# Attention scores against 64 keys instead of 128, each batch's result in a PSUM bank of its own

## The chip, the cores and the metric

The kernel runs on one core of a Trainium2 chip. The metric is the device time of one launch in microseconds (us); the number given for a kernel is the median of its runs.

## The reference, cut to what matters

The program is a GRU scan, an attention layer over the GRU's states, a Runge-Kutta integration and a quantized feed-forward layer, with residuals between them. The change lies in the attention:

```python
q = (xn @ Wq)...          # 32 batches, 16 heads, 64 positions, 128 wide
k, v = kv[..., :dh], kv[..., dh:]          # one key and value head for all 16
q, k = rotary(q) * scale, rotary(k)
sim = einsum('bhid,bjd->bhij', q, k)       # 64 x 64 for each batch and head
sim = where(causal, -max_float, sim)
attn = softmax(sim - max(sim))
out = einsum('bhij,bjd->bhid', attn, v)
```

A query meets the 64 keys of its own batch and no others.

## The kernel before, in words

Five engines run programs of their own and meet by semaphores. The stages follow one another: the GRU (0 to about 380 us of the span), attention (about 389 to 1008 us), then Runge-Kutta and feed-forward together to the end.

**Attention** goes over 8 blocks (`NBLK`) of 4 batches (`BLK_B`), 256 tokens. A block is 2 pairs (`PAIRS`) of batches, since two batches of 64 positions fill 128 partitions. All operands of its matmuls are float32, for which the profile records two weight loads and two matmuls for each `matmul` in the program. TensorE's order of work is written out by hand in `attn_block` of the tensor program. For each block:

- keys of the block (L667), values (L671), then the queries of the 16 heads (L656, 64 matmuls of 256 columns). VectorE rotates the heads as they come (L1180, L1182, L1197) into `q_rot`, laid out as batch, head, position; the rotated keys are in `kr`, 256 columns, 64 for each batch.
- `before(0)`: a quarter of the output projection of the block before (8 matmuls of 512 columns, L646, 16 records).
- `scores(0)` (L681 to L691): for each batch of pair 0, 8 matmuls, one for each pair of heads. The weights are the 128 query columns of two heads (`q_rot`), and the moving operand is 128 keys: those of both batches of the pair. A batch's 8 results fill two PSUM banks: banks 2 and 3 for the pair's first batch, 4 and 5 for its second. Half of each result (the keys of the other batch) is not used. One semaphore (`s_mm`) is raised after each batch.
- `before(1)`, then `scores(1)` into the same banks 2 to 5; for that, TensorE first waits until VectorE has read out the earlier batch of those banks (`masked`, L685).
- `turned_probs(0)` (transposes, L701), `before(2)`, `values(0)` (L714), `turned_probs(1)`, `before(3)`, `values(1)`. `values` puts its results into banks 5, 2 and 3, after all four batches of the block were read (`masked`).

In the first block there is no output projection, so the parts `before(...)` are empty.

VectorE's `softmax(blk, pr)` works on the two batches of a pair in turn: for each batch it adds the causal mask while reading the batch's own keys out of PSUM (L1213), takes the maximum (L1216), subtracts it (L1219); ScalarE takes the exponential (L936); VectorE sums (L1222), inverts (L1225) and scales (L1228), and raises `p_done`, for which `turned_probs` waits. After both pairs VectorE normalizes the next block's input (L1165, L1170) and adds the residual of the last (L1234). ScalarE copies the turned probabilities (L943) and the attention's output (L948) out of PSUM.

The read of the scores in `softmax` is this view: two banks, head by head, 64 of each 128 columns.

```python
own = ps[:, 2 + 2 * (n % 2):4 + 2 * (n % 2), :].rearrange(
    "p a (h b j) -> p (a h) b j", b=2, j=T)[:, :, n % 2, :]
```

Of the kernel before, what the change touches and what calls it, by code (L numbers as in the profile page):

```python
# [13 lines left out]
P = 128  # L14
B, T, D = 32, 64, 512
# [8 lines left out]
PAIRS = BLK_B // 2  # L24
# [113 lines left out]
def gru_attn_rk4_ffn(nc, xT, x, cond_quad, cond_T, W_ih, W_hh, gate_bias, state_bias, gamma, Wq, Wkv, Wo,  # L138
                     couplingT, bias_quad, w_gate, w_up, w_down, down_idx, ident, mean_of, trig, mask,
                     x1_scr, q_scr, wgu_scr, wd_scr, scale_scr, tok_scr, out):  # L140
    with ExitStack() as ctx:
        mem = ctx.enter_context(nc.sbuf_tensor("mem", [P, WORDS], F32))
        ps = ctx.enter_context(nc.psum_tensor("ps", [P, 8, 512], F32))
# [4 lines left out]
        def f32(a, *dims):  # L148
            n = 1
            for d in dims:  # L150
                n *= d
            v = mem[:, a:a + n]
            if len(dims) == 2:
                v = v.rearrange("p (a b) -> p a b", a=dims[0])
            if len(dims) == 3:
                v = v.rearrange("p (a b c) -> p a b c", a=dims[0], b=dims[1])
            return v
# [24 lines left out]
        q_rot = f32(a_ih, BLK_B, HEADS * T)  # L182
# [7 lines left out]
        kr, kturned = f32(w.take(BLK), BLK), f32(w.take(BLK), BLK)  # L190
# [379 lines left out]
        def _(pe):  # L570
# [67 lines left out]
            def out_proj(blk, part):  # L638

                pr, h0 = part // 2, part % 2 * HP  # L640
                if h0 == 0:

                    pe.wait_ge(x1_done, PRIMED + PAIRS * (blk - 1) + pr + 1)
                    pe.wait_ge(ao_cp, 4 * (PAIRS * blk + pr + 1))
                for h in range(h0, h0 + HP):
                    mm = pe.matmul(ps[:, 6 + pr, :], aoT[:, h, pr * P:pr * P + P], wo[:, h, :], start=(h == 0), stop=(h == HEADS - 1))  # L646
                if h0:
                    mm.then_inc(wo_mm, 1)

            def q_heads(blk):  # L650
                for h in range(HEADS):
                    if h >= Q_BANKS:

                        pe.wait_ge(q_ev, 3 * (HEADS * blk + h - Q_BANKS + 1))
                    for c in range(NC):
                        mm = pe.matmul(ps[:, h % Q_BANKS, 0:BLK], wq[:, c, h * DH:(h + 1) * DH], xnb[:, c, :], start=(c == 0), stop=(c == NC - 1))  # L656
                    mm.then_inc(q_mm, 1)

            def attn_block(blk, first):
                pe.wait_ge(xn_done, blk + 1)  # L660
                if not first:

                    pe.wait_ge(x1_done, PRIMED + PAIRS * (blk - 1))
                    pe.wait_ge(pT_cp, 2 * PAIRS * blk)
                    pe.wait_ge(ao_cp, 4 * PAIRS * blk)
                for c in range(NC):
                    mm = pe.matmul(ps[:, 7, 0:BLK], wkv[:, c, 0:DH], xnb[:, c, :], start=(c == 0), stop=(c == NC - 1))  # L667
                mm.then_inc(k_mm, 1)
                for pr in range(PAIRS):
                    for c in range(NC):  # L670
                        mm = pe.matmul(ps[:, 5, pr * DH:(pr + 1) * DH], xnb[:, c, pr * P:pr * P + P], wkv[:, c, DH:], start=(c == 0), stop=(c == NC - 1))  # L671
                mm.then_inc(v_mm, 1)
                q_heads(blk)
                pe.wait_ge(kr_done, blk + 1)

                def before(part):

                    if not first:
                        out_proj(blk - 1, part)

                def scores(pr):  # L681
                    for b2 in range(2):
                        if pr:

                            pe.wait_ge(masked, 2 * PAIRS * blk + 2 * pr - 1 + b2)  # L685
                        b = 2 * pr + b2
                        for hp in range(HP):

                            o = ps[:, 2 + 2 * b2 + hp // 4, (hp % 4) * P:(hp % 4 + 1) * P]
                            mm = pe.matmul(o, q_rot[:, b, hp * P:(hp + 1) * P], kr[:, pr * P:(pr + 1) * P], start=True, stop=True)  # L690
                        mm.then_inc(s_mm, 1)  # L691

                def turned_probs(pr):
                    pe.wait_ge(p_done, 2 * (PAIRS * blk + pr + 1))
                    for half in range(2):

                        n = 2 * pr + half
                        if n >= 2:
                            pe.wait_ge(pT_cp, 2 * PAIRS * blk + n - 1)
                        for hp in range(4 * half, 4 * half + 4):  # L700
                            mm = pe.transpose(ps[:, half, (hp % 4) * P:(hp % 4 + 1) * P], probs[:, pr, hp * P:(hp + 1) * P], identf)  # L701
                        mm.then_inc(pT_mm, 1)

                def values(pr):
                    pe.wait_ge(pT_cp, 2 * PAIRS * blk + 2 * pr + 2)

                    pe.wait_ge(masked, 2 * PAIRS * (blk + 1))
                    for half in range(2):
                        for b2 in range(2):
                            n = 4 * pr + 2 * half + b2  # L710
                            if n >= 3:

                                pe.wait_ge(ao_cp, 4 * PAIRS * blk + n - 2)
                            pe.matmul(ps[:, PV_BANKS[n % 3], :], vtok[64 * b2:64 * b2 + 64, pr, :], pT[64 * b2:64 * b2 + 64, half * 512:(half + 1) * 512],  # L714
                                      start=True, stop=True).then_inc(pv_mm, 1)
                before(0)
                pe.wait_ge(qr_done, HEADS * (blk + 1))
                pe.wait_ge(v_cp, blk + 1)
                scores(0)
                before(1)  # L720
                scores(1)
                turned_probs(0)
                before(2)
                values(0)
                turned_probs(1)
                before(3)
                values(1)
# [104 lines left out]
            for bank in range(2):  # L832

                mm = pe.matmul(ps[:, bank, 0:P], identf, mix[0], start=True, stop=True)
# [200 lines left out]
        def _(dve):  # L1035
            def bcast(row, nb):

                return row.unsqueeze(1).to_broadcast([P, nb, T])
# [160 lines left out]
            def softmax(blk, pr):  # L1199

                def of(n):
                    return probs[:, pr, :].rearrange("p (h b j) -> p h b j", h=HP, b=2)[:, :, n % 2, :]

                def row(a, n):
                    return a[:, n, :].unsqueeze(2).to_broadcast([P, HP, T])

                def at(n):
                    return 2 * PAIRS * blk + n + 1
                two = (2 * pr, 2 * pr + 1)
                for n in two:  # L1210
                    dve.wait_ge(s_mm, at(n))
                    own = ps[:, 2 + 2 * (n % 2):4 + 2 * (n % 2), :].rearrange("p a (h b j) -> p (a h) b j", b=2, j=T)[:, :, n % 2, :]
                    dve.tensor_tensor(of(n), own, bcast(masks, HP), ALU.add).then_inc(masked, 1)  # L1213
                for n in two:
                    dve.wait_ge(masked, at(n))
                    dve.tensor_reduce(smax[:, n, :], of(n), AX.X, ALU.max).then_inc(max_done, 1)  # L1216
                for n in two:
                    dve.wait_ge(max_done, at(n))
                    dve.tensor_tensor(of(n), of(n), row(smax, n), ALU.subtract).then_inc(shifted, 1)  # L1219
                for n in two:  # L1220
                    dve.wait_ge(exp_done, at(n))
                    dve.tensor_reduce(ssum[:, n, :], of(n), AX.X, ALU.add).then_inc(sum_done, 1)  # L1222
                for n in two:
                    dve.wait_ge(sum_done, at(n))
                    dve.reciprocal(ssum[:, n, :], ssum[:, n, :]).then_inc(inv_done, 1)  # L1225
                for n in two:
                    dve.wait_ge(inv_done, at(n))
                    dve.tensor_tensor(of(n), of(n), row(ssum, n), ALU.mult).then_inc(p_done, 1)  # L1228
# [7 lines left out]
            def attn_block(blk, first, last):  # L1236
                dve.wait_ge(k_mm, blk + 1)
                rotated(by_time(kr), by_time(kturned), by_time(ps[:, 7, 0:BLK]), 2, k_parts)
                dve.wait_ge(k_parts, 3 * (blk + 1))
                dve.tensor_tensor(kr, kr, kturned, ALU.add).then_inc(kr_done, 1)  # L1240
                q_out(blk)
                for pr in range(PAIRS):
                    softmax(blk, pr)
                if first:

                    dve.wait_ge(rows_ld, 32)
                if not last:
                    norm(blk + 1)
                if not first:
                    residual(blk - 1)  # L1250
# [307 lines left out]
```

## Time and profile before

| what | value |
|---|---|
| median of 3 runs | 1623.13 us (1622.98 to 1623.77) |
| the profiled execution's own time | 1630.71 us |
| its span, first to last instruction | 1628.8 us |
| TensorE matmuls (PE) busy | 1505.1 us, 92% of the span |
| TensorE weight loads (PEld) busy, beside the matmuls | 933.8 us, 57% |
| VectorE (DVE) busy | 1122.3 us, 69% |
| ScalarE (ACT) busy | 591.0 us, 36% |
| GpSimd (POOL) busy | 383.0 us, 24% |
| mean granted TensorE clock | 0.975 of full speed |

Line numbers (L690) are those of the kernel. PE stands for matmuls and PEld for the loads of their stationary operand, both on TensorE. Durations of matmuls overlap, because they are pipelined; the time that a stream of them takes is read from a stretch, not from the duration of one. "Idle" is what stood before an instruction on its engine, with what ended it. PEclk is the TensorE clock that the throttle granted: 1.0 is 2.4 GHz, 0.5 is 1.2 GHz.

### The profile page before, as it was taken

The page shows a single profiled execution, that of the slowest core. Times are in us where ns is not written, and L with a number is a line of the kernel's source. Part 1 is how long each engine was busy: PE and PEld are TensorE (multiplying, and loading weights), DVE is VectorE, ACT ScalarE, POOL GpSimd, SP SyncE. Part 2 cuts the span into 40 slices and gives each one's busy share as a digit, 9 for nine tenths or more (in the row PEclk, how much of TensorE's full clock was granted, in tenths as well). Part 3 has the DMA queues.
Part 4 walks back from the last instruction along what each step waited for, and adds up shares of the span by engine and source line. Part 5 has one row for each costly group of instructions (what it writes and reads, how often), then busy time and mean ns, then how long its engine had stood idle before and what let it go on. Part 6 is the DMA issues. An engine that isn't in the chain of part 4 may idle for free.

```text
span 1628.8 us, 46380 instructions
## 1 busy us (share of the span) xinstructions
PE 1505.1 (92%) x16624; PEld 933.8 (57%) x16624; DVE 1122.3 (69%) x3565; ACT 591.0 (36%) x1903; POOL 383.0 (24%) x545
## 2 busy tenths in 40 slices
PE   5999999996799999999999998789999999999995
PEld 1333333334675758576766753566666666666662
DVE  1676667765755747575756541578889898898886
ACT  1444445451111020202011110455655555555552
POOL 0221221120000000000000000235556655555650
PEclk9999999998889999999999999999999999999996
DMA  7111211216100000000000004201111111111111
GB/s 306 45 45 50 51 47 56 61 47 168 10 1 8 19 13 13 26 0 26 0 26 1 25 6 167 73 24 30 37 32 35 34 48 40 32 35 35 32 44 39
DMA packets 91035, 72.79 MB, mean 45 GB/s; under 512 B 32480, under 2 KB 82912, under 8 KB 89824
## 3 DMA queue, kind: packets, MB, share of 16 engines
q1 hardware_dynamic: 71184, 59.35, 12.4%
q10 hardware_dynamic: 18032, 6.88, 1.7%
q0 software_dynamic: 1760, 5.77, 1.3%
q8 instruction: 37, 0.61, 0.2%
q14 instruction: 22, 0.18, 0.0%
HBM read 55.03 MB, written 16.94 MB: 44 GB/s over the span
## 4 chain that ended last, share of the span: by engine, by line
PE 68%; DVE 14%; issue 7%; POOL 5%; ACT 4%; DMA 1%; POOLq 0%; DVEq 0%; SPq 0%; ACTq 0%
PE ps L656 14%; PE ps L646 14%; PE ps L584 11%; PE ps L596 10%; PE ps L751 7%; PE ps L690 3%; PE ps L714 3%; DVE mem L1327 2%; POOL mem L532 2%; DVE mem L1278 2%; ACT mem L969 2%; POOL mem L514 2%; PE ps L741 1%; DVE ps L1303 1%; PE ps L667 1%
## 5 line engine op out<-in xcount | busy, mean ns | idle before, releaser
L751 PE MATMUL ps<-mem 128*32 128x128 f32 x8192 | 278.8, 277 | 38.9 <-ACT mem L969 32.9
L751 PEld LDWEIGHTS ps<-mem 128*32 128x32 f32 x8192 | 211.6, 110 | 109.5 <-ACT mem L969 68.9
L646 PE MATMUL ps<-mem 128*128 128x512 f32 x512 | 224.6, 592 | 0.0
L656 PE MATMUL ps<-mem 128*128 128x256 f32 x1024 | 222.3, 379 | 0.0
L510 POOL TENSOR_TENSOR mem<-mem 128x128 f32<-128x128 f32 x64 | 39.6, 618 | 743.3 <-ACT mem L964 743.3
L656 PEld LDWEIGHTS ps<-mem 128*128 128x128 f32 x1024 | 193.9, 190 | 26.0
L584 PE MATMUL ps<-mem 128*32 128x384 f32 x2048 | 181.3, 496 | 9.7 <-DMA mem<-in_W_ih 5.8
L596 PE MATMUL ps<-mem 128*32 128x384 f32 x2048 | 177.6, 487 | 2.4 <-DVE mem L1106 2.4
L936 ACT ACTIVATE mem<-mem 128x512 f32<-128x512 f32 x32 | 19.7, 630 | 392.4 <-DVE mem L1219 392.4
L646 PEld LDWEIGHTS ps<-mem 128*128 128x128 f32 x512 | 95.6, 190 | 109.7 <-issue 109.3
L969 ACT ACTIVATE mem<-mem 128x64 f32<-128x64 f32 x512 | 109.9, 250 | 118.8 <-DVE mem L1278 112.2
L741 PE MATMUL ps<-mem 128*128 128x128 f32 x768 | 137.5, 302 | 10.0 <-DVE ps L1303 8.6
L741 PEld LDWEIGHTS ps<-mem 128*128 128x128 f32 x768 | 100.6, 191 | 52.0 <-DVE ps L1303 26.1
L961 ACT ACTIVATE ps<-mem 128x128 f32<-128x128 f32 x256 | 72.0, 281 | 160.8 <-DVE mem L1327 160.6
L514 POOL TENSOR_TENSOR mem<-mem 128x128 f32<-128x128 f32 x192 | 97.0, 505 | 133.7 <-ACT mem L964 127.6
L596 PEld LDWEIGHTS ps<-mem 128*32 128x32 f32 x2048 | 62.7, 110 | 109.0 <-issue 80.6
L584 PEld LDWEIGHTS ps<-mem 128*32 128x32 f32 x2048 | 64.3, 112 | 105.8 <-issue 91.1
L1182 DVE TENSOR_TENSOR mem<-ps,mem 64x256 f32<-64x256 f32 x272 | 114.7, 422 | 8.5
L1180 DVE TENSOR_TENSOR mem<-ps,mem 128x256 f32<-128x256 f32 x136 | 57.8, 425 | 75.5 <-PE ps L667 45.4
L767 PE MATMUL ps<-mem 128*128 128x352 bf16 x512 | 100.1, 321 | 3.9 <-DVE mem L1451 3.4
L481 POOL COPY mem<-mem 128x128 f32 (+1 forms) x64 | 37.7, 589 | 275.9 <-DVE mem L1106 275.9
L964 ACT ACTIVATE mem<-mem 128x128 f32<-128x128 f32 x320 | 87.8, 293 | 0.0
(139 smaller groups left out, 2115.9 us busy)
## 6 DMA issues: line engine op xcount, KB each, us to landing
mem<-x_scr SPq DMA_DIRECT2D x128, 64.0 KB, 1.9
mem<-in_xT SPq DMA_DIRECT2D x64, 64.0 KB, 2.2
mem<-in_Wq SPq DMA_DIRECT2D x1, 4096.0 KB, 12.2
mem<-in_Wo SPq DMA_DIRECT2D x1, 4096.0 KB, 20.1
mem<-in_x SPq DMA_DIRECT2D x16, 256.0 KB, 2.8
x_scr<-mem SPq DMA_DIRECT2D x32, 128.0 KB, 2.3
q_scr<-mem SPq DMA_DIRECT2D x64, 64.0 KB, 1.6
mem<-q_scr SPq DMA_DIRECT2D x64, 64.0 KB, 1.9
```

The source lines that it names most:

```text
L514: tt(pacc, pacc, pw[1 + st], ALU.add).then_inc(rk_pa, 1)
L584: mm = pe.matmul(ps[32 * j:32 * j + 32, par, 0:3 * P].rearrange("p (g n) -> p g n", g=3), xt[par][:, c, :], wih[:, c, :].rearrange("p (g j ...
L596: mm = pe.matmul(ps[32 * j:32 * j + 32, par, P:4 * P].rearrange("p (g n) -> p g n", g=3), hT[1 - par][:, c, :], whh[:, c, :].rearrange("p ...
L646: mm = pe.matmul(ps[:, 6 + pr, :], aoT[:, h, pr * P:pr * P + P], wo[:, h, :], start=(h == 0), stop=(h == HEADS - 1))
L656: mm = pe.matmul(ps[:, h % Q_BANKS, 0:BLK], wq[:, c, h * DH:(h + 1) * DH], xnb[:, c, :], start=(c == 0), stop=(c == NC - 1))
L741: pe.matmul(ps[:, st % 2, 0:P], mix[m], (None, qn[(s - 1) % 4], *qst)[k], start=False, stop=False, skip_group_check=True)
L751: mm = pe.matmul(ps[32 * j:32 * j + 32, st % 2, 0:P], thT[:, c, :], ct[:, c, j * P:(j + 1) * P], start=False, stop=(c == NC - 1), skip_gro ...
L767: mm = pe.matmul(ps[:, 2 + order % 2, 0:GU_N], qxT[:, c, :], (wgT if gate else wuT)[:, c, m * GU_N:(m + 1) * GU_N], start=(c == 0), stop=( ...
L961: act.activation(ps[:, 5, 0:P], src, ACT.Square, scale=(STEP[st] / 3) ** 0.5).then_inc(rk_sq, 1)
L964: act.activation(pw[of], (pn[(s - 1) % 2], src)[of > 0], ACT.Copy, scale=float(weight)).then_inc(rk_w, 1)
L969: act.activation(thT[:, 2 * half:2 * half + 2, :], qsT[:, 2 * half:2 * half + 2, :], ACT.Tanh).then_inc(rk_th, 1)
L1182: dve.tensor_tensor(share[b:b + DH // 2], src[a:a + DH // 2], bcast(trigs[:, tr + 1, :], BLK_B)[a:a + DH // 2], ALU.mult).then_inc(done, 1)
```

## The change

Each batch's queries meet only the 64 columns of `kr` that hold that batch's keys, so the moving operand has 64 columns in place of 128. The 8 results of a batch then take 512 columns, one bank, and batch b of the block writes bank 2 + b. The wait for `masked` in `scores` is gone, since no bank is written twice in it. VectorE reads one whole bank in place of half the columns of two. The number of matmuls, their weights and every other line stay.

```diff
                 def scores(pr):
                     for b2 in range(2):
-                        if pr:
-
-                            pe.wait_ge(masked, 2 * PAIRS * blk + 2 * pr - 1 + b2)
                         b = 2 * pr + b2
                         for hp in range(HP):
-
-                            o = ps[:, 2 + 2 * b2 + hp // 4, (hp % 4) * P:(hp % 4 + 1) * P]
-                            mm = pe.matmul(o, q_rot[:, b, hp * P:(hp + 1) * P], kr[:, pr * P:(pr + 1) * P], start=True, stop=True)
+                            mm = pe.matmul(ps[:, 2 + b, hp * T:(hp + 1) * T], q_rot[:, b, hp * P:(hp + 1) * P], kr[:, b * T:(b + 1) * T],
+                                           start=True, stop=True)
                         mm.then_inc(s_mm, 1)
...
                 for n in two:
                     dve.wait_ge(s_mm, at(n))
-                    own = ps[:, 2 + 2 * (n % 2):4 + 2 * (n % 2), :].rearrange("p a (h b j) -> p (a h) b j", b=2, j=T)[:, :, n % 2, :]
+                    own = ps[:, 2 + n, :].rearrange("p (h j) -> p h j", j=T)
                     dve.tensor_tensor(of(n), own, bcast(masks, HP), ALU.add).then_inc(masked, 1)
```

## Rows read from the trace of the kernel before

**Rows 1.** The page: busy time and instructions of each engine; TensorE's clock in 40 slices.

```profile
PE 1505.1 (92%) x16624; PEld 933.8 (57%) x16624; DVE 1122.3 (69%) x3565; ACT 591.0 (36%) x1903; POOL 383.0 (24%) x545
...
PEclk9999999998889999999999999999999999999996
```

**Rows 2.** Busy time by stretch, blocks 1 to 7 of attention; below it, TensorE's waits there.

```profile
core 0: us, PE busy (x) PEld busy (x) DVE busy (x) ACT busy (x) POOL busy (x), PEclk, DMA share, GB/s
464.00:990.00 526.00, 521.88 (x2187) 354.23 (x2187) 316.68 (x702) 72.44 (x125) 0.00 (x0) 1.00 0.06 18
...
PE ps L667 <- ACT mem L948: 4.1, 6, 0.7
```

**Rows 3.** The chain of waits in order of time, one block: start us, us, what.

```profile
573.27 3.57 PE ps L690 x32
576.84 6.87 PE ps L646 x16
583.71 3.57 PE ps L690 x32
587.28 0.87 PE ps L701 x8
588.15 6.87 PE ps L646 x16
595.02 2.86 PE ps L714 x8
```

**Rows 4.** Groups by line, 464 to 990 us: matmuls and weight loads of the scores.

```profile
L690 PE MATMUL ps<-mem 128*128 128x128 f32 x448 | 52.3, 275 | 0.0
L690 PEld LDWEIGHTS ps<-mem 128*128 128x128 f32 x448 | 52.2, 192 | 6.7 <-issue 6.7
```

**Rows 5.** Line L701 (transposes, also 128 columns): duration ns min/median/max, first and last start.

```profile
L701 PEld LDWEIGHTS ps<-mem x128: 137/141/231, 439.6 to 970.2; 128*128 128x128 f32 x128
L701 PE MATMUL ps<-mem x128: 270/272/477, 439.6 to 970.3; 128*128 128x128 f32 x128
```

**Rows 6.** Timeline of L633 and L635 (start, us): full weights, 64 columns; L633's durations below.

```profile
377.90 0.30 PEld L633 LDWEIGHTS ps<-mem 128*128 128x128 f32 x2 [5.10 <-issue]
377.93 0.41 PE L633 MATMUL ps<-mem 128*128 128x64 f32 x2 [4.43 <-ACT mem L855]
379.30 0.69 PE L635 MATMUL ps<-mem 128*128 128x64 f32 x2 [0.96 <-DVE mem L1149]
...
L633 PEld LDWEIGHTS ps<-mem x2: 186/188/189, 377.9 to 378.0; 128*128 128x128 f32 x2
L633 PE MATMUL ps<-mem x2: 275/284/294, 377.9 to 378.1; 128*128 128x64 f32 x2
L635 PE MATMUL ps<-mem x2: 422/449/476, 379.3 to 379.6; 128*128 128x64 f32 x2
```

**Rows 7.** Timeline of VectorE in the same block, and the residual's read of PSUM, L1234.

```profile
575.09 0.69 DVE L1213 TENSOR_TENSOR mem<-ps,mem 128x512 f32<-128x512 f32 x1 [4.22 <-PE ps L690]
576.88 0.69 DVE L1213 TENSOR_TENSOR mem<-ps,mem 128x512 f32<-128x512 f32 x1 [1.10 <-PE ps L690]
581.49 1.28 DVE L1228 TENSOR_TENSOR mem<-mem 128x512 f32<-128x512 f32 x2
...
L1234 DVE TENSOR_TENSOR mem<-ps,mem x16: 680/690/692, 521.7 to 1008.0; 128x512 f32<-128x512 f32 x16
```

**Rows 8.** The chain of waits in order of time, block 0 (selected lines).

```profile
426.91 6.73 PE ps L690 x32
433.64 0.02 issue
433.67 0.69 DVE mem L1213
...
438.36 1.20 DVE mem L1228 x2
439.56 1.20 DVE mem L1213 x2
...
443.72 1.07 ACT mem L943 x2
```

**Rows 9.** Busy time by stretch, same columns as rows 2: TensorE's clock at selected times.

```profile
377.80:378.40 0.60, 0.41 (x2) 0.30 (x2) 0.03 (x1) 0.60 (x1) 0.00 (x0) 1.00 0.95 216
379.00:385.00 6.00, 0.69 (x2) 0.50 (x2) 3.30 (x11) 1.83 (x4) 0.00 (x0) 0.50 0.12 35
427.00:433.00 6.00, 6.00 (x28) 6.00 (x29) 0.69 (x1) 0.00 (x0) 0.00 (x0) 0.50 0.01 3
444.00:464.00 20.00, 17.79 (x46) 10.43 (x47) 6.59 (x17) 7.82 (x13) 0.00 (x0) 0.51 0.00 0
1030.00:1040.00 10.00, 6.90 (x156) 5.41 (x159) 5.73 (x27) 4.66 (x21) 2.18 (x6) 1.00 0.06 15
```

## The prediction

> **What bounds the kernel now.** I read the page first. TensorE's matmuls are busy 92% of the span, VectorE 69%, and the clock is at 0.9 or above but for a dip to 0.8 in slices 11 and 12, where attention begins [rows 1]. Busy PE is no proof, so I took the stretch in which the changed lines run: in blocks 1 to 7 of attention (464 to 990 us) PE is busy 521.88 of 526.00 us, at full clock, and its only wait there is 4.1 us, for ScalarE [rows 2]. So in these seven blocks the end is set by the pace at which TensorE works its queue, and a microsecond taken out of that queue is a microsecond of the kernel. The chain of one block shows the two stretches that change: 3.57 us of scores, twice, each 32 records (16 matmuls of the program, two records each) [rows 3]. Block 0 is another case: the chain leaves TensorE after the first 32 records of scores and goes through the softmax on VectorE [rows 8].
>
> **The part that is meant to pay: 64 columns in place of 128.** The count of matmuls and of weight loads stays; half of the moving columns go. The pitch of the stream is 3.57 / 32 = 0.1116 us a record [rows 3]. What sets it, the 128 moving columns or the 128 columns of weights behind them? If the columns alone set it, 128 of them would cost a quarter of the 512-column records: 6.87 / 16 = 0.429 us, a quarter is 0.107 [rows 3]. Both are near, so I look for what tells them apart.
>
> First, the weight loads fill the stretch: their 448 records keep the load path busy 52.2 us, the matmuls 52.3 us [rows 4]. A load's record is 192 ns long and they start each 112 ns, so a record is longer than its place in the stream, and I need the distance of two loads that nothing holds back.
>
> Second, that distance. L633 loads full 128 x 128 weights twice and sends 64 columns through each: the very form that the change makes. Its two loads together last 0.30 us, one is 0.186 to 0.189, so the second starts 0.11 us after the first. Its two matmuls start at 377.93 and end at 378.34; the first is 0.275 or 0.294 long, so it ends at 378.205 or 378.224, and the second ends 0.12 to 0.135 us later [rows 6], at full clock [rows 9]. Were the 64 columns the limit, that would be about 0.056. L635, the same form at half clock [rows 9], says the same: the end at 379.99, the first end at 379.722 or 379.776, 0.21 to 0.27 us apart [rows 6], where scores of 128 columns at half clock have 6.00 / 28 = 0.214 [rows 9]. Half the columns, no shorter pitch, at either clock.
>
> Third, the transposes of L701 move 128 columns too, but their loads are shorter (141 against 192 ns), and their pitch is 0.87 / 8 = 0.109, a little under 0.1116 [rows 3 to 5]. That fits scores that already wait for their weights, by some 2 to 3 ns each.
>
> So the scores are bound by the load of the queries, which the change leaves alone. I take 0.1116 us a record after the change, and 0.109 as the low end (the transposes' pitch): in blocks 1 to 7 that is 7 x 64 = 448 records by 0 to 0.0026 us, a gain of 0 to 1.2 us. I take 0, as L633 has nothing under 0.11. Two rules of the Trainium skill pull apart here. "TensorE: Matmul & The Clock Gate", section "LDWEIGHTS (loading the stationary operand)", has a load take the number of its columns over 1.2 GHz, 107 ns for 128, whatever is sent through: by it the sum stays 0, and the 0.11 us of L633 agrees. The same page's section "Back-to-back issue gap" counts about 60 cycles for up to 64 columns against 134 for 128: that one gives the first rival.
>
> **The wait taken away.** In blocks 1 to 7 TensorE has 6.87 us of projection between the two stretches, and VectorE has read the second batch at 576.88 + 0.69 = 577.57, six microseconds before the second stretch starts at 583.71 [rows 3, 7]. The wait was passed at once; gone, it gives 0. In block 0 nothing lies between, and masking the second batch ended at 433.67 + 0.69 = 434.36 [rows 8]; even a wait there would have given nothing back, since TensorE idles after the scores until `p_done` at 438.36 + 1.20 = 439.56 [rows 8]. 0 again, and no wait is added. Banks 2, 3 and 5, which `values` uses, still wait for all four reads, and bank 5's value half was copied out before (the wait for `v_cp` stays).
>
> **VectorE's read.** One bank in a row in place of half the columns of two. The strided read takes 0.69 us [rows 7], the contiguous read of a bank in the residual has a median of 0.690 [rows 7]. Between -0.01 and +0.01 us for each of 32; in blocks 1 to 7 it lies beside TensorE's queue: `p_done` comes at 581.49 + 1.28 = 582.77 and the transposes that need it start at 587.28, 4.5 us of cover [rows 3, 7]. In block 0 it is on the chain: four times 0.01, nothing.
>
> **Block 0.** Its first 32 records of scores run at half clock in 6.73 us and start the softmax [rows 8]. At an unchanged pitch they stay. The last matmul of a batch is shorter by 64 columns, so `s_mm` comes 0.05 us sooner, 0.1 at half clock: a gain of 0.1 us. The clock is the unknown. It rose during the scores (0.50 from 427 to 433 [rows 9]); with half the columns it may rise later or elsewhere. If it stayed at half throughout, 64 records by 0.214 would end at 440.6, 1.0 us after `p_done`, and the chain behind, VectorE's masks of pair 1 first and then the copies at 443.72 [rows 8], would come up to 1.0 us later. In the other direction 444 to 464 runs at half clock [rows 9]; were a shift in the clock to give back a sixth of these 20 us, that is 3.3 us. Bounds: -3.3 to +1.0, I take 0.
>
> **Sum:** 0 - 0 - 0.1 = -0.1 us against the profiled execution's 1630.71 us, whose span is 1628.8. That execution stands 7.6 us over the median of 1623.13; as a difference, the sum carries over: 1623.0 us. About 0.2%, 3.2 us, is what a measurement of this kernel can tell from no change; the forecast is no change.
>
> **Rival 1: the columns set the pace, faster.** If 64 columns go at half the pitch, 0.0558 us, each block saves 64 x 0.0558 = 3.57 us, seven blocks 25.0. It would not be swallowed: the softmax of pair 0 would start some 1.8 us sooner, the transposes 3.57 us sooner, and of the 4.5 us of cover [rows 3, 7] 2.7 would be left. Block 0 gains half of the 6.73 us [rows 8], 3.4. Together 28.4: 1594.7 us. For it: the stated gap for small matmuls (named above), and that the quarter of a 512-column record, 0.107, lies so near 0.1116. Against it: both pairs of 64 columns [rows 6]. They are pairs, not a stream, which is why I leave it 7 in 100. A pitch between the two would give part of the 28.4.
>
> **Rival 2: the clock falls, slower.** After the change the multiplying array gets columns half of the time in a 3.57 us stretch, and the second stretch runs straight into the transposes. If the throttle took that for rest, 32 records of scores would cost 0.214 - 0.1116 = 0.102 us more each, 3.3 us, and 8 transposes as much again each, 0.8: 4.1 a block, 28.7 in seven blocks, 1651.8 us. It decides once PEclk falls under 1.00 in 464 to 990 us. For it: in block 0 the clock stayed at 0.51 from 444 to 464 though PE was busy 17.79 of 20 us [rows 9]. Against it: from 1030 to 1040 us PE is busy 6.90 of 10 us, with 32-column weights and gaps, at clock 1.00 [rows 9], and 6.87 us of full columns precede each stretch [rows 3]. I give it 5 in 100.
>
> **How the numbers follow.** No change 88 in 100, rival 1 (whole or in part) 7, rival 2 5. The predicted time is that of no change, 1623.0. Its bounds are -1.2 (pitch 0.109) and -3.3 (block 0's clock) below, +1.0 above, and 0.6 for the spread of the runs on either side, one microsecond more for what I did not see: 1618.0 to 1625.5. Both rivals lie outside and hold 12 in 100, which may be left out. A little of the forecast's own low end is over 0.2%: faster 0.09, same 0.86, slower 0.05.
>
> **What would show it.** In the profile of the changed kernel: the stretch of 32 records of scores still 3.5 to 3.6 us in the chain; mean PEld of that line at 190 ns and its busy time about 52 us; matmul records still about 275 ns, as in L633 [rows 6], or shorter by 64 columns (0.429 / 8 = 54 ns), which would not tell the cases apart; PE's only wait in blocks 1 to 7 still the 4 us for ScalarE; PEclk 1.00 there. A stretch of about 1.8 us makes rival 1 right and my reading of L633 wrong; a clock under 1.00 or a stretch over 4 us, rival 2; VectorE's L1213 off 0.69 by more than 0.05, the costing of the read.

## The result, and the profile after

| kernel | median | runs | ratio to before, 95% interval |
|---|---|---|---|
| before | 1623.85 us | 20 (1621.97 to 1631.03) | |
| changed | 1630.88 us | 20 (1627.57 to 1633.5) | 1.0037 (1.003 to 1.0044) |

Slower by 0.37%, some 7 us, where I had forecast no change and a range up to 1625.5. The profiled execution of the changed kernel took 1628.55 us, less than the first profiled one of before (1630.71). So these two profiles alone show a gain where the medians show a loss, and the first question is which of them is typical.

First what went as the steps said. The chain of the same block as in [rows 3], the changed kernel:

```profile
571.34 3.52 PE ps L685 x32
574.86 6.92 PE ps L646 x16
581.78 3.52 PE ps L685 x32
585.30 0.88 PE ps L697 x8
586.18 6.87 PE ps L646 x16
```

The stretch of scores is 3.52 us against 3.57. The projection behind the first stretch takes 6.92 against 6.87 and gives that back, so about 0.05 us a block is won: from the keys of one block to the keys of the next (L667 in the chain) it is 607.36 - 533.07 = 74.29 us here and 609.33 - 535.00 = 74.33 before. Groups by line from 464 to 990 us of the changed kernel (columns as in [rows 4]):

```profile
L685 PEld LDWEIGHTS ps<-mem 128*128 128x128 f32 x448 | 52.2, 192 | 6.7 <-issue 6.7
L685 PE MATMUL ps<-mem 128*128 128x64 f32 x448 | 51.5, 273 | 0.0
...
L1209 DVE TENSOR_TENSOR mem<-ps,mem 128x512 f32<-128x512 f32 x28 | 19.4, 692 | 63.8 <-PE ps L685 63.8
```

Its busy time by stretch (columns as in [rows 2]):

```profile
464.00:990.00 526.00, 521.88 (x2182) 353.16 (x2181) 316.73 (x702) 72.08 (x124) 0.00 (x0) 1.00 0.07 20
```

And all of TensorE's waits there:

```profile
PE ps L667 <- ACT mem L944: 4.1, 6, 0.7
```

Loads as busy as before (52.2 us, [rows 4]), matmuls 0.8 us less, the mask 0.69 us, clock 1.00, the one wait unchanged. Blocks 1 to 7 lost nothing. The loss must stand elsewhere. Here is block 0 of the changed kernel, the chain of waits in order of time, for comparison with [rows 8]:

```profile
427.44 13.90 PE ps L685 x64
441.34 0.02 issue
441.37 0.69 DVE mem L1209
...
445.02 1.07 ACT mem L939 x2
...
446.13 4.83 PE ps L710 x8
450.96 1.91 PE ps L697 x8
...
453.55 4.56 PE ps L710 x8
...
458.78 1.99 PE ps L667 x8
460.78 1.78 PE ps L671 x16
462.56 1.08 PE ps L656 x5
```

All 64 records of the scores run at 13.90 / 64 = 0.217 us, the pitch of half clock. In the first profile of before the clock rose within the scores, after some 28 of the 64 records (to be compared with 427 to 433 in [rows 9]):

```profile
433.00:437.00 4.00, 4.00 (x38) 4.00 (x36) 3.24 (x6) 0.82 (x2) 0.00 (x0) 1.00 0.00 0
```

That profile, however, fell back to half clock for the rest of the block, as [rows 9] show from 444 to 464. Was that usual?

### The profile page after: what moved, and what is told of

Its sections match the earlier page's. It is cut to its first block, busy times and chain, and to the rows that moved or that the text cites. A ratio compares the mean times of both kernels' runs of the same rounds, so it can differ in the third digit from the quotient of the medians.

```text
span 1626.6 us, 46332 instructions
## 1 busy us (share of the span) xinstructions
PE 1500.3 (92%) x16583; PEld 935.6 (58%) x16624; DVE 1122.8 (69%) x3565; ACT 590.9 (36%) x1903; POOL 383.5 (24%) x545
## 4 chain that ended last, share of the span: by engine, by line
PE 67%; DVE 15%; issue 7%; POOL 5%; ACT 4%; DMA 1%; POOLq 0%; DVEq 0%; SPq 0%; ACTq 0%
PE ps L656 14%; PE ps L646 14%; PE ps L584 11%; PE ps L596 10%; PE ps L747 6%; PE ps L685 4%; PE ps L710 3%; DVE mem L1323 3%; DVE mem L1274 2%; POOL mem L532 2%; ACT mem L965 2%; DVE ps L1299 2%; POOL mem L514 2%; DVE mem L1421 1%; DVE mem L1380 1%
## 5 line engine op out<-in xcount | busy, mean ns | idle before, releaser
L656 PE MATMUL ps<-mem 128*128 128x256 f32 x1024 | 222.3, 379 | 0.0
L656 PEld LDWEIGHTS ps<-mem 128*128 128x128 f32 x1024 | 193.9, 190 | 26.0
```

## The experiments

**A second look at both kernels.** No edit. 

> The kernel before, unchanged, for a second profile and for the granted clock of many executions. The first profile took 1630.71 us where the median is about 1623.9. Theory A (TensorE's clock in block 0 of attention): a typical execution of before has less half-clock time between 389 and 464 us than the first profile had, a mean clock of about 0.98 in place of 0.975, and a time of 1623 to 1625 us. Rival B (the difference lies after attention, in Runge-Kutta and feed-forward): the clock of attention is as in the first profile, and the missing 7 us are found after 1016 us.

> The changed kernel, unchanged. Its 20 runs fall into two groups, 1627.6 to 1628.7 us at a mean clock of 0.974 to 0.975 and 1630.9 to 1633.5 at 0.967 to 0.969. Theory A: both groups have the scores of block 0 wholly at half clock (64 records in 13.9 us), and the slower group has one more stretch at half clock. Rival B: the groups differ after attention. Time 1627 to 1633 us, ratio to before 1.003 to 1.004.

Before again: 1624.14 us in 12 runs, its profiled execution 1624.75; changed again: 1632.44 us in 8 runs, 1.004 (1.0023 to 1.0057), its profiled execution 1634.12. Block 0 of before in its second profile, the chain of waits:

```profile
429.10 5.45 PE ps L690 x32
...
444.63 1.07 ACT mem L943 x2
...
445.75 4.47 PE ps L714 x8
450.22 0.60 PE ps L701 x4
...
452.07 2.95 PE ps L714 x8
...
455.69 2.00 PE ps L667 x8
457.68 1.78 PE ps L671 x16
459.46 0.65 PE ps L656 x3
```

Compare the second `values` stretch (L714): 2.95 us, where it is 4.56 in the changed kernel (L710). From the first score to the first query matmul of block 1 (L656) before takes 459.46 - 429.10 = 30.4 us here and 464.44 - 426.91 = 37.5 in the first profile. The difference of 7.1 us is about what the first profile stood over the median (6.9). Busy time by stretch, the second profile of before, then of the changed kernel (columns as in [rows 2]; the figure behind POOL's is PEclk):

```profile
427.00:442.00 15.00, 10.10 (x72) 9.71 (x72) 9.93 (x20) 1.23 (x2) 0.00 (x0) 0.89 0.00 1
442.00:464.00 22.00, 16.74 (x70) 11.08 (x71) 11.65 (x28) 9.41 (x16) 0.00 (x0) 0.84 0.00 1
```

```profile
427.00:442.00 15.00, 12.72 (x61) 12.75 (x61) 8.41 (x17) 1.23 (x2) 0.00 (x0) 0.58 0.00 1
442.00:464.00 22.00, 17.53 (x46) 9.88 (x46) 9.43 (x21) 9.24 (x15) 0.00 (x0) 0.51 0.00 0
```

A clock of 0.89 over 15 us is 2 x 0.11 x 15 = 3.3 us at half. Worked out so, these second profiles have some 10 us at half clock in these 37 us before the change and some 34 after it. Theory A held in its core. Of its details one missed: the changed kernel's two groups of runs differ less in block 0 (35.1 and 36.6 us to the first query) than I had expected. The slower profile also enters block 0 1.8 us later, though that alone does not mark a slow execution (the faster profile of before enters it 2.2 us later than the slower one), and it has a lower clock from 1020 to 1200 us (0.96 against 0.99 in the faster).

Part of the loss stands ahead of the copies (L943, L939 in the changed kernel), for which `values` waits: from the first score to the copies it is 17.6 us in the changed kernel (445.02 - 427.44) and 15.5 in the second profile of before (444.63 - 429.10), because the first 32 records take some 7 us at half clock (5.45 there) and the last mask has to wait for the 64th, which ends at 441.34. These are 2.0 us; the rest stands behind the copies.

**Where the loss is: one part of the kernel each.**

```diff
                 def scores(pr):
+                    narrow = first
...
-                        if pr:
+                        if pr and (not narrow or False):
...
                             pe.wait_ge(masked, 2 * PAIRS * blk + 2 * pr - 1 + b2)
...
+                            if narrow:
+                                mm = pe.matmul(ps[:, 2 + b, hp * T:(hp + 1) * T], q_rot[:, b, hp * P:(hp + 1) * P], kr[:, b * T:(b + 1) * T],
+                                               start=True, stop=True)
+                                continue
...
+                    if narrow:
+                        own = ps[:, 2 + n, :].rearrange("p (h j) -> p h j", j=T)
...
-                    softmax(blk, pr)
+                    softmax(blk, pr, first)
```

This is the edit that changes block 0 alone; for blocks 1 to 7 alone `first` is `not first` in both places.

> 64 columns, banks and missing wait in block 0 of attention only; blocks 1 to 7 as before. Theory A: the whole loss is here, 1627 to 1633 us, ratio 1.003 to 1.005, with the scores of block 0 at half clock for all 64 records. Rival C (the new bank layout, or 64 columns in the PE-bound blocks, costs in blocks 1 to 7): 1623 to 1624.5 us, no difference from before.

> 64 columns in blocks 1 to 7 only; block 0 as before. Theory A: the loss is gone and the small gain of the pitch stays (3.52 for 3.57 us a stretch, 14 stretches, 0.7 us): 1622.5 to 1624.5 us, ratio 0.999 to 1.0005. Rival C: 1628 to 1632 us.

The change in block 0 alone: 1632.36 us, 1.0044 (1.0029 to 1.0059), the whole loss. In blocks 1 to 7 alone: 1625.13 us, 1.0004 (0.9994 to 1.0014), nothing. The 0.7 us that I had put on the shorter stretches did not come, and the time lies 0.6 us over the range expected: the gain of a block's first stretch is given back behind it, as shown above, so about 0.05 us a block is left, which no median here can show. The same two stretches, first of the change in block 0 alone, then in blocks 1 to 7 alone:

```profile
427.00:442.00 15.00, 12.52 (x59) 12.55 (x60) 8.20 (x18) 1.23 (x2) 0.00 (x0) 0.58 0.01 1
442.00:464.00 22.00, 17.53 (x46) 9.94 (x46) 9.80 (x21) 9.24 (x15) 0.00 (x0) 0.50 0.00 0
```

```profile
427.00:442.00 15.00, 9.88 (x72) 9.49 (x72) 10.24 (x20) 1.30 (x3) 0.00 (x0) 0.85 0.01 1
442.00:464.00 22.00, 18.30 (x78) 12.61 (x79) 11.64 (x28) 9.27 (x16) 0.00 (x0) 0.87 0.00 1
```

**Columns or wait?**

```diff
+                    narrow = True
...
-                        if pr:
+                        if pr and (not narrow or True):
```

> The changed kernel with the wait for masked put back (64 columns and a bank for each batch stay). Theory A (with 64 columns the scores of block 0 do not raise the clock): as slow as the changed kernel, 1628 to 1633 us, the scores of block 0 at half clock for all 64 records. Rival D (the missing wait lets the second pair's scores disturb the first pair's softmax): back to 1623 to 1625 us.

1629.79 us, 1.0035 (1.002 to 1.005), with 13.90 us for the 64 records of block 0. Putting the wait back returns nothing of the loss; rival D falls. The 64 columns and their banks remain together. No row speaks for the bank as a cause, but the two were not parted.

**What sets the pitch of the scores.** In both kernels below block 0 is as before, blocks 1 to 7 are changed and part of the work is left out, as the expectations say.

```diff
-mm = pe.matmul(ps[:, 2 + b, hp * T:(hp + 1) * T], q_rot[:, b, hp * P:(hp + 1) * P], kr[:, b * T:(b + 1) * T],
+mm = pe.matmul(ps[0:T, 2 + b, hp * T:(hp + 1) * T], q_rot[:, b, hp * P:hp * P + T], kr[:, b * T:(b + 1) * T],        # half_weights
+mm = pe.matmul(ps[:, 2 + b, hp * T:hp * T + T // 4], q_rot[:, b, hp * P:(hp + 1) * P], kr[:, b * T:b * T + T // 4],  # few_columns
```

> Block 0 as before. In blocks 1 to 7 the scores load 64 weight columns (one head of each two) and send 64 columns; the scores of every second head are left out, so the output is not the reference's. If the load of 128 weight columns sets the pitch of the scores after the change (0.110 us a record), it falls to 0.055 to 0.065 here, a stretch of 32 records takes 1.8 to 2.1 us in place of 3.52, and 14 stretches save 20 to 24 us: 1600 to 1605 us. Rival E (an issue cost of each record sets the pitch): 3.5 us a stretch, 1624 us.

> Block 0 as before. In blocks 1 to 7 the scores keep their 128 weight columns and send 16 columns in place of 64; three quarters of the scores are left out, so the output is not the reference's. If the load sets the pitch: 3.5 us a stretch as with 64 and 128 columns, 1623 to 1626 us unless the clock falls in blocks 1 to 7. Rival F (columns still count under 64): shorter than 3.4 us a stretch, under 1621 us.

Half the weight columns: 1605.09 us, 0.9884 (0.9869 to 0.9899). Groups by line from 464 to 990 us of that kernel:

```profile
L690 PE MATMUL ps<-mem 128*64 128x64 f32 x448 | 29.1, 223 | 0.0
L690 PEld LDWEIGHTS ps<-mem 128*64 128x64 f32 x448 | 27.2, 138 | 10.6 <-issue 10.6
```

One stretch in its chain of waits:

```profile
564.71 2.01 PE ps L690 x32
```

A stretch takes 2.01 us, 0.063 a record, against 3.52 with 128 weight columns and the same 64 moving ones. So with 128 weight columns the load sets the pitch, and an issue cost for each record (rival E) does not. That 0.063 is more than half of 0.110 is not explained by these runs.

Sixteen moving columns: 1650.52 us, 1.0145 (1.0114 to 1.0177), 26 us slower for a quarter of the columns (three of four runs at 1650 to 1652, one at 1639.51). The expectation had named a fall of the clock as the exception, without a time for it. Its busy time by stretch, blocks 1 to 7:

```profile
464.00:990.00 526.00, 521.88 (x2105) 354.74 (x2104) 313.55 (x696) 67.56 (x116) 0.00 (x0) 0.95 0.05 13
```

Its chain of waits in one block:

```profile
569.65 4.20 PE ps L690 x32
573.85 9.61 PE ps L646 x16
583.46 4.32 PE ps L690 x32
587.78 1.79 PE ps L705 x8
589.56 8.49 PE ps L646 x16
```

Here the clock falls within blocks 1 to 7, and the dear part is not the scores (4.20 us against 3.52) but the projection behind them, 9.61 us against 6.87 at full clock. It is my rival 2 in its place, for 16 columns where I had put it for 64. That the 26 us lie near its 28.7 is luck: I had priced the scores and the transposes, and most of the price is paid in the projection. Rival F cannot be judged by this stretch, since part of it runs at half clock.

Block 0 of these two kernels still has 128 columns, and their profiles show it as the second profile of before does: PEclk 0.89 from 427 to 442 and 0.84 from 442 to 464 in both.

**Holding the clock.** If the clock is the cost, full matmuls in TensorE's gaps of block 0 must bring the time back. The fillers' results are not used.

```diff
+            def kept_warm(n, bank=6):
+                for _ in range(n):
+                    pe.matmul(ps[:, bank, :], identf, wq[:, 0, 0:512], start=True, stop=True)
...
+                if first:
+                    kept_warm(5)
                 before(0)
                 pe.wait_ge(qr_done, HEADS * (blk + 1))
                 pe.wait_ge(v_cp, blk + 1)
                 scores(0)
                 before(1)
                 scores(1)
+                if first:
+                    kept_warm(2)
                 turned_probs(0)
+                if first:
+                    kept_warm(4)
                 before(2)
                 values(0)
                 turned_probs(1)
+                if first:
+                    kept_warm(1)
                 before(3)
```

> The changed kernel with twelve filler matmuls of 512 columns in block 0 (results unused, into bank 6, which is free there), placed where TensorE waits: 5 before the scores, 2 after them, 4 after the first transposes, 1 after the second. Theory A: the clock stays at 1.0 from about 392 us through block 0, the scores of block 0 take 7 us in place of 13.9, and the time falls under that of the kernel before: 1614 to 1621 us, ratio 0.994 to 0.999. Rival G (the clock level in block 0 is not what costs): the fillers change nothing or delay block 0, 1628 us or more.

> The changed kernel with only the 5 filler matmuls before the scores of block 0. Theory A, refined (half the columns cannot raise the clock, but they can hold it): the scores start at full clock and the 64 records take about 7.2 us in place of 13.9; the clock falls later, at the gaps after them, as it does in the kernel before. 1621 to 1626 us, about the kernel before. Rival H (half the columns cannot even hold the clock in block 0): it falls within the scores, 1627 us or more.

> The kernel before (128 columns) with the twelve fillers in block 0. The remaining half-clock stretches of block 0 (3.4 and 6.8 us in the second profile of before) go: 1618 to 1623 us. Against warm_after, whose median is 1622.62, it shows what the 64 columns are worth once the clock is held: theory says 0.7 us for 14 stretches, so the two should not be told apart.

Twelve fillers on the changed kernel: 1622.62 us, 0.9986 (0.9977 to 0.9995), 8 us under the changed kernel's 1630.88 by work added, though a little over the 1621 expected. Its profiled execution, 1618.95, is the fastest of its 11 runs, eight of which lie from 1621.7 to 1623.7; block 0 of those was not seen. Rival G falls. The same on the kernel before: 1621.05 us, 0.9984 (0.9972 to 0.9996); the two cannot be told apart. With only the five fillers ahead of the scores (warm_lead) the scores run at full clock and most of the rest doesn't: 1628.45 us, 1.0017 (1.0002 to 1.0031), above what I had expected. Four of its ten runs lie from 1622.6 to 1625.0, the other six from 1628.2 to 1630.3, and the profiled one is of these six. Its busy time by stretch:

```profile
427.00:442.00 15.00, 9.32 (x72) 8.79 (x72) 11.63 (x22) 2.99 (x6) 0.00 (x0) 0.84 0.00 1
442.00:464.00 22.00, 20.13 (x59) 12.48 (x60) 6.49 (x18) 7.87 (x13) 0.00 (x0) 0.56 0.00 1
```

Its chain of waits:

```profile
427.50 3.80 PE ps L690 x32
...
442.50 4.83 PE ps L715 x8
...
449.91 4.84 PE ps L715 x8
```

Half the columns hold the clock here when they begin with it, which is A's picture; the time is H's, because the clock fell in the gaps after the scores and, in this profile, stayed down. The scores' own pitch costs nothing here: the copies follow the first score as fast as with the clock held throughout. What costs is the 4.8 us for each `values` in place of 2.9, and keys and values of block 1 behind them.

**A version that beats both.**

```diff
+            pe.wait_ge(w_att, 32)
+            kept_warm(4)
             pe.wait_ge(part_done, 2 * T)
...
-            pe.wait_ge(w_att, 32)
+            kept_warm(9)
             attn_block(0, True)
...
             for part in range(2 * PAIRS):
                 out_proj(NBLK - 1, part)
+            kept_warm(7, bank=0)
```

> The changed kernel with the twelve fillers of block 0, and fillers in the three other gaps round attention: 4 before the token means, 9 before block 0's keys, 7 after the last output projection (bank 0, free there). The half-clock stretches at 378 (13.7 us) and 1000 us (10.2 us) should mostly go; behind them stand 3.8 us of keys and values and the first Runge-Kutta stages. 1613 to 1620 us, faster than warm_after by 2 to 6 us. If the fillers run past the end of their waits, it gives back up to 3 us.

> The kernel before (128 columns, two banks for each batch) with all the fillers of warm_all. If the 64 columns are worth only the 0.05 us for each of 14 stretches once the clock is held, this is within 1 us of warm_all (1617.81 us): 1616.5 to 1619.5 us. If half the columns cost clock elsewhere too, it is faster than warm_all by over 2 us; if they gain more than the pitch shows, slower by over 2 us.

With fillers in the gaps round attention too, the changed kernel takes 1617.81 us, 0.9959 (0.9945 to 0.9972), the kernel before 1617.86 us, 0.9943 (0.9929 to 0.9958). Both are 6 us or more under either kernel without fillers, and the two are not told apart: their medians agree, and their ratios, each against runs of before beside it, have overlapping intervals. Busy time by stretch of the first of the two, whose profiled execution (1620.72) is the slowest of its five runs:

```profile
378.00:389.00 11.00, 9.32 (x21) 3.90 (x21) 4.47 (x17) 3.92 (x8) 0.40 (x1) 0.84 0.42 119
...
427.00:464.00 37.00, 34.97 (x181) 25.36 (x182) 24.51 (x53) 10.54 (x18) 0.00 (x0) 1.00 0.00 0
```

All of block 0 side by side: the clock, and the time from the first score to the first query matmul of block 1, worked out from each chain as above.

| kernel | PEclk 427 to 442 | PEclk 442 to 464 | us to block 1's queries | profiled execution, us | median us |
|---|---|---|---|---|---|
| before, first profile | 0.73 | 0.51 | 37.5 | 1630.71 | 1623.85 |
| before, second profile | 0.89 | 0.84 | 30.4 | 1624.75 | 1624.14 |
| changed, first profile | 0.50 | 0.64 | 35.1 | 1628.55 | 1630.88 |
| changed, second profile | 0.58 | 0.51 | 36.6 | 1634.12 | 1632.44 |
| changed in block 0 alone | 0.58 | 0.50 | 38.2 | 1634.01 | 1632.36 |
| changed in blocks 1 to 7 alone | 0.85 | 0.87 | 30.0 | 1625.00 | 1625.13 |
| changed, with the wait | 0.54 | 0.50 | 38.3 | 1631.36 | 1629.79 |
| changed, five fillers | 0.84 | 0.56 | 34.5 | 1628.24 | 1628.45 |
| changed, twelve fillers | 1.00 | 1.00 | 27.2 | 1618.95 | 1622.62 |

## Why the prediction was wrong

**Right: the pitch.** "I take 0.1116 us a record after the change, and 0.109 as the low end": measured 3.52 / 32 = 0.110, and the load shown as its cause. The two records of L633 were enough to tell it. Rival 1 is out. The Trainium skill, "TensorE: Matmul & The Clock Gate", section "LDWEIGHTS (loading the stationary operand)", gives the time of a load as its columns over 1.2 GHz; estimates from that rule are 107 ns for 128 columns and 53 ns for 64. The traces have 110 and 63 ns a record: near for 128, a little over for 64. The table of about 60 cycles in the section "Back-to-back issue gap" of the same page is given there for an isolated matmul, without its load. It does not describe this stream, whose 64 moving columns took 110 ns a record, so these runs neither bear it out nor refute it.

**Right: the wait and VectorE's read.** The wait put back changed nothing of note, and each mask takes 0.69 us as before.

**Wrong: the step "Block 0".** It said that the clock might rise later, bounded that at +1.0 us and took 0. Two things failed. First the value taken: with 64 columns the scores of block 0 did not raise the clock in either profile of the changed kernel (13.9 and 13.7 us for 64 records), so the case that I held as a bound is the usual one. Second the bound itself. For what it covered it was right: from the first score to the copies it is 17.6 us now and was 443.72 - 426.91 = 16.8 in the profile that I read, 0.8 more. But there I stopped, as if the rest of the block had to run at half clock in any case. It did in that profile [rows 9], and against it the changed block 0 even looks short (35.1 and 36.6 us against 37.5). It does not in the second profile of before, where the block from first score to block 1's queries takes 30.4 us. Against that one the changed kernel loses 35.1 - 30.4 = 4.7 us and 36.6 - 30.4 = 6.2 in its two profiles, and 38.2 - 30.4 = 7.8 with the change in block 0 alone; the medians differ by 7.0. So the term that I set at 0 is some 5 to 8 us, and about 2 of them stand ahead of the copies.

**What stood in sight.** The prediction noted that the profiled execution was 7.6 us over the median, and let the sum carry over "as a difference". It does not carry over if what makes an execution slow is what the change makes usual: a block 0 mostly at half clock. Of the 25 runs of before timed beside the first experiments 23 lie between 1621.8 and 1627.53 and two at 1630.7, like that profile; that these two also had the low clock in block 0 is likely but was not seen. The changed kernel has its first 20 runs from 1627.57 up, and one of the 8 later ones at 1625.78.

**Rival 2 was the right mechanism in the wrong place.** Its point of decision, a clock under 1.00 in 464 to 990 us, was not reached with 64 columns and was reached with 16. In blocks 1 to 7, 6.87 us of full columns stand before each stretch of scores; block 0 has none: TensorE idles 4.9 us before its first score, and the clock falls to half within a microsecond of that score. I had put the risk where the clock was high, and the change took effect where it was low. That the full columns ahead of the scores are what holds the clock in blocks 1 to 7 fits this and was not tested.

**Smaller slips.** The terms named for the range add up to 1623.0 - 1.2 - 3.3 - 0.6 - 1.0 = 1616.9 below and 1625.6 above, not 1618.0 and 1625.5; the result lies outside either. And the clock in [rows 1] is below 0.9 in slices 10 to 12, and 0.6 in the last, not in 11 and 12 alone.

**Open.** Why the changed kernel's runs fall into two groups, about 3 us apart, is not settled: its slower profile differs in the time of the first score (429.28 against 427.44) and in the clock from 1020 to 1200 us. Nor was the bank layout parted from the columns. Why the clock came back in block 0 after the scores in one profile of before and not in the other is open too.

## What to carry to other kernels

Before cutting the moving columns of a matmul, look whether its weight load already fills the pitch; if so, nothing is won, and columns that cost no time may be what brings the clock back up. When a change thins out TensorE's work, look for effects where the clock is about to rise or fall, not where it is steady, and price a late clock up to where it rises again. When the profiled execution stands away from the median by as much as the effect in question, take another profile first.

## What the runs showed of the hardware that I had not expected

TensorE was busy with scores without a gap for 13.9 us at half clock and the granted clock did not rise: 14.56 of 15.00 us busy at 0.50 in the changed kernel's first profile, for 64 moving columns behind 128 weight columns. The same holds for all four profiles with 64 columns in block 0 and no fillers. In all five with 128 moving columns there and no fillers, it rose 3 to 6 us after the first score. With sixteen columns, also without a gap in the scores, it did not stay up: the mean over blocks 1 to 7 was 0.95, where it was 1.00 with 64. So a busy PE in the profile does not by itself tell the clock to come. And with matmuls whose results nobody reads, in the gaps of TensorE, the changed kernel stands 6.8 us under the kernel before (1617.81 against 1624.62 in runs side by side), where without them it is 7 us over.
